# Third block's self-attention: two loops with the choice of queries between them, or one stream with the choice behind it

## The chip, the cores and the metric
The kernel runs on one core of one Trainium2 chip. A core has five engines with queues of their own: TensorE (PE in the profile, its weight loads PEld), VectorE (DVE), ScalarE (ACT), GpSimd (POOL) and SyncE (SP), which only starts DMAs here. The metric is the time of the whole kernel on the device, in microseconds: the median of three runs.

## The reference, cut to what matters
The network has twelve layers (four blocks of cross-attention, self-attention and feed-forward); x is 64 sequences of 32 tokens of 128 numbers. The layer in question adds to x the following, computed from the layer-normed x:

```python
Q, K, V = proj(wq, bq), proj(wk, bk), proj(wv, bv)        # 16 heads of 8
scores = jnp.einsum('bhqd,bhkd->bhqk', Q, K) * scale
u = min(L, max(1, int(np.log(L))))                        # 3 of 32 queries
top_u = jax.lax.top_k(scores.max(axis=-1), u)[1]          # the 3 with the highest maximum, per sequence and head
q_sel = jnp.take_along_axis(Q, top_u[..., None], axis=2)
attn = jax.nn.softmax(jnp.einsum('bhud,bhkd->bhuk', q_sel, K) * scale, axis=-1)
ctx = jnp.einsum('bhuk,bhkd->bhud', attn, V)
padded = zeros.at[bi, hi, top_u].set(ctx)                 # the other 29 queries give zero
return padded.transpose(0, 2, 1, 3).reshape(B, L, D) @ wo.T + bo
```

## The kernel before
All is float32. The 2048 tokens are 16 tiles of 128 rows (four sequences each) and four quarters of four tiles. Layers run one after the other. Every engine has its own program of the whole network, written out in order; between them stand counting semaphores (`T.done` counts one up, `T.due` lists what still has to be waited for). An engine takes its instructions strictly in order, so an instruction that waits holds everything behind it. At the end of a layer each engine drains, and the next layer begins when all have (`fence_before`). PSUM has eight banks of 512 columns; the dictionary `free` says for each bank which event must have come before PE writes it again.

The layer is `L2Attn` (line 2625). All projections and scores of a sequence and head are computed for all 32 queries, and the choice is a mask of zeros and ones.

Start (`start_pe`, line 589): PE turns the normed rows of quarters 0 to 2 (line 388), fills the gap until quarter 3 is normed with query projections (line 424, two passes per matmul), turns quarter 3, and projects the last quarter's queries and all keys. ACT empties the even quarters (line 438), DVE the odd ones (line 450).

First loop, 16 tiles: POOL spreads the keys of a tile by head (`pool_keys`, line 1670, four operations); PE computes the scores of 16 heads into four banks, two sets of banks in turn (`pe_scores`, line 1491, 32 passes); DVE takes the maximum over the keys (line 1552) and subtracts it (line 1555); ACT takes exp in place (line 1628); DVE adds up the weights (line 2708). The weights of all 16 tiles are kept.

Then the choice (line 2654 on): PE turns the 16 x 16 maxima of each row so that a partition holds (tile, head) and a row holds the 32 queries of a sequence; DVE copies them (line 2711) and finds the three highest in three rounds of six or seven small operations (`pick_dve`, line 508); takes the reciprocal of all 256 sums per row (line 2715); PE turns the mask back; DVE multiplies it into the reciprocals (line 2719).

Second loop, 16 tiles: POOL multiplies the weights by that gate (line 1678); ACT repeats the normed x of a sequence four times (line 1612); PE computes the values at full width, four matmuls into 512 columns (line 1505), turns the weights of a tile (line 1514) and averages (line 1524, 32 small passes); DVE adds the bias to the values and masks them (lines 1581 and 1585); ACT copies the turned weights (line 1635) and the average (line 1642). PE's order in a step is values of tile i, turn of tile i-1, average of tile i-2.

Output: PE multiplies by the output weights per quarter (line 460), DVE adds the bias (line 553) and adds to x (line 556).

`HeadStream` (line 1692) is the form that three other layers use: lines 1736 (scores), 1750 (values, 32 small passes straight into one row block per head), 1760 (turn), 1771 (average, with four more columns per group that give the sums of the weights), DVE 1805 and 1808, ACT 1849 (four copies of the values), 1874 (exp) and 1880 (copy of the turned weights), POOL 1894 (keys). In it a divided mean is turned back per tile (lines 1815, 1818, 1779, 1856).

Other lines that the prediction speaks of: 368 is a matmul that only keeps PE busy, 551 and 556 are additions to x.

Of the kernel before, what the change touches and what calls it, by code (L numbers as in the profile page):

```python
# [10 lines left out]
ALU = mybir.AluOpType  # L11
# [32 lines left out]
class Tally:  # L44
# [8 lines left out]
    def sem(self, name):  # L53
# [15 lines left out]
        "z": "lin_out", "z_out": "lin_out", "rows": "rows_out", "ffn_hidden": "lin_out", "products": "lin_out",  # L69
# [1383 lines left out]
class HeadAttention:  # L1453

    def __init__(self, g, tag, room, qT, kT, ready, xT, wv, scale, OT, *, key_mask=None, block=None, softcap=None,
                 bias_col=None, bias_row=None, repeated=None, keepall=False):
        self.g, self.tag, self.qT, self.kT, self.ready, self.xT = g, tag, qT, kT, ready, xT
        self.wv, self.scale, self.OT, self.key_mask, self.block = wv, scale, OT, key_mask, block  # L1460
        self.softcap, self.bias_col, self.bias_row, self.repeated = softcap, bias_col, bias_row, repeated
        self.keepall = keepall
        self.kB = [room.take(BT * HG * S) for _ in range(3)]
        if repeated is None:
            self.xR = [room.take(BT * HG * S) for _ in range(3)]
        self.pr = [room.take(H, S) for _ in range(NT if keepall else 3)]
        self.pT = [room.take(NG * P) for _ in range(2)]
        self.vB = [room.take(BT * D) for _ in range(3)]
        self.mx, self.sm = room.take(NT, H), room.take(NT, H)
        self.rest = room  # L1470

    def output(self, q):
        return "h_out", (self.tag, 4 * q + 3)

    def score_bank(self, i):
        return NG * (i % 2) if self.keepall else 0

    def tile(self, i):
        return self.repeated[i] if self.repeated is not None else self.xR[i % 3]

    def pe_scores(self, e, T, free, i):
        g, PS, at0 = self.g, self.g.PS, self.score_bank(i)
        for w in T.due(*free_of(free, at0), ("h_keys", (self.tag, i)), *self.ready(i // 4)):
            e.wait_ge(*w)
        for n in range(NG):
            r = slice(S * n, S * n + S)
            for b in range(BT):
                at = P * i + S * b  # L1490
                k = e.matmul(PS[S * b:S * b + S, at0 + n, 0:P], self.qT[r, at:at + S], self.kB[i % 3][r, P * b:P * b + P],
                             start=True, stop=self.key_mask is None)
        for n in range(NG if self.key_mask is not None else 0):
            k = e.matmul(PS[:, at0 + n, 0:P], self.block, spread(self.key_mask(i), [P, HG, S], 1), start=False, stop=True)
        k.then_inc(*T.done("h_scores", (self.tag, i)))
        free[at0] = ("h_less" if self.softcap is None else "h_tanh"), (self.tag, i)
        for n in range(1, NG):
            free[at0 + n] = free[at0]

    def pe_values(self, e, T, free, i):  # L1500
        PS, b, x = self.g.PS, 4 + i % 2, self.tile(i)
        for w in T.due(free[b], ("h_repeated", (self.tag if self.repeated is None else "shared", i))):
            e.wait_ge(*w)
        for j in range(BT):
            k = e.matmul(PS[:, b, D * j:D * j + D], x[:, P * j:P * j + P], self.wv, start=True, stop=True)
        k.then_inc(*T.done("h_values", (self.tag, i)))
        free[b] = ("h_biased" if self.bias_row is not None else "h_masked"), (self.tag, i)

    def pe_turn(self, e, T, free, i):
        PS, p = self.g.PS, self.pr[i % len(self.pr)].rearrange("p (g h) k -> p g (h k)", g=NG)  # L1510
        for w in T.due(free[6], ("h_normal", (self.tag, i))):
            e.wait_ge(*w)
        for n in range(NG):
            k = e.transpose(PS[:, 6, P * n:P * n + P], p[:, n, :], self.g.C["ident"])
        k.then_inc(*T.done("h_turned", (self.tag, i)))
        free[6] = ("h_pT", (self.tag, i))

    def pe_average(self, e, T, free, i):
        PS = self.g.PS
        for w in T.due(free[7], ("h_pT", (self.tag, i)), ("h_masked", (self.tag, i))):  # L1520
            e.wait_ge(*w)
        for j in range(BT):
            for n in range(NG):
                k = e.matmul(PS[S * n:S * n + S, 7, S * j:S * j + S], self.vB[i % 3][:, D * j + S * n:D * j + S * n + S],
                             self.pT[i % 2][:, P * n + S * j:P * n + S * j + S], start=True, stop=True)
        k.then_inc(*T.done("h_average", (self.tag, i)))
        free[7] = ("h_out", (self.tag, i))

    def pe(self, e, T, free, fill=None):
        for i in range(NT + 2):  # L1530
            if i < NT:
                self.pe_scores(e, T, free, i)
                self.pe_values(e, T, free, i)
# [3236 lines left out]
```

## Time and profile before

| what | value |
|---|---|
| timed runs | 2098.18, 2100.51, 2100.89 us; median 2100.51 |
| the profiled execution | 2076.97 us, span 2075.2 us |
| granted clock of TensorE, mean | 0.911 of 2.4 GHz |
| PE busy | 1733.9 us, 84% of the span |
| DVE busy | 1371.5 us, 66% |
| ACT busy | 1035.9 us, 50% |
| POOL busy | 916.9 us, 44% |
| DMA | 130.63 MB moved |
| first score of the layer | 987.41 us from the start of the span |
| its last addition begins | 1070.08 us |

The profile is of one execution. "Chain" is the chain of work that ended last, followed back from the last instruction; "issue" in it is time in which an engine waited for nothing that the profile shows. PE's granted clock has two levels here, 1.00 (2.4 GHz) and 0.50 (1.2 GHz); a number between them in a window means that it changed inside. A float32 matmul appears as two passes.

### The profile page before, as it was taken

To read this page: it belongs to the slowest core of one execution; us is meant where nothing else is said; L and a number is where in the kernel's file an instruction comes from. 1 tells how busy PE (TensorE), PEld (TensorE's weight loads), DVE (VectorE), ACT (ScalarE), POOL (GpSimd) and SP (SyncE) were. 2 spreads that over 40 slices of the span, in tenths; PEclk is the share of its full clock that TensorE was granted. 3 is DMA by queue.
4 is the path that set the end of the run, shared out by engine and by line. 5 is a ranking of instruction groups with operands and counts; after the bars stand their busy time and mean duration, and the time that the engine had idled before them with its cause. 6 is when DMAs were issued, how large, how long until landed. Compare 5 with 4: busy or idle time off the path is not lost.

```text
span 2075.2 us, 49700 instructions
## 1 busy us (share of the span) xinstructions
PE 1733.9 (84%) x19776; PEld 1173.8 (57%) x19776; DVE 1371.5 (66%) x3589; ACT 1035.9 (50%) x2670; POOL 916.9 (44%) x1092
## 2 busy tenths in 40 slices
PE   7678999999988789988387879999999997547596
PEld 4323556666654656654265756677766675125396
DVE  6799996576765555446883168666777866676622
ACT  4445664488864742233231346676766753115243
POOL 2243454556650624210533053216767668423543
PEclk9878999999999999999597989999999998766698
DMA  8000000100017100053004411100001000031187
GB/s 358 1 1 0 0 1 1 76 5 5 5 36 314 66 2 1 1 209 138 2 25 141 136 29 25 38 21 12 21 12 31 11 11 1 10 136 45 53 303 234
DMA packets 60424, 130.63 MB, mean 63 GB/s; under 512 B 16713, under 2 KB 38940, under 8 KB 54560
## 3 DMA queue, kind: packets, MB, share of 16 engines
q1 hardware_dynamic: 56896, 121.32, 16.2%
q0 software_dynamic: 3296, 6.12, 0.9%
q8 instruction: 157, 2.57, 0.5%
q14 instruction: 75, 0.61, 0.1%
HBM read 107.97 MB, written 20.12 MB: 62 GB/s over the span
## 4 chain that ended last, share of the span: by engine, by line
PE 54%; DVE 22%; issue 8%; ACT 7%; DMA 4%; POOL 3%; SPq 1%; POOLq 1%; DVEq 0%; ACTq 0%
PE PS L3254 4%; PE PS L2541 4%; PE PS L424 3%; PE PS L460 3%; PE PS L3301 3%; PE PS L3286 2%; PE PS L3285 2%; DMA arena<-in_ctx 2%; PE PS L3243 2%; PE PS L1760 2%; PE PS L2341 2%; PE PS L1736 2%; DVE arena L253 2%; PE PS L1082 1%; PE PS L3293 1%
## 5 line engine op out<-in xcount | busy, mean ns | idle before, releaser
L321 POOL TENSOR_TENSOR arena<-arena 128x4 f32<-128x4 f32 (+3 forms) x109 | 118.8, 1091 | 365.3 <-DVE arena L264 243.9
L3369 ACT ACTIVATE arena<-PS,arena 128x289 f32<-128x289 f32 x256 | 127.6, 503 | 73.5 <-DVE arena L3483 73.1
L3483 DVE TENSOR_REDUCE arena<-PS 128x1 f32<-128x289 f32 x256 | 113.6, 455 | 71.7 <-PE PS L3254 67.6
L3254 PE MATMUL PS<-arena 128*128 128x289 f32 x512 | 150.6, 417 | 10.4 <-ACT arena L3369 7.5
L1894 POOL TENSOR_TENSOR arena<-arena 128x128 f32<-128x128 f32 x384 | 140.4, 403 | 38.0 <-PE PS L1736 16.5
L1258 POOL TENSOR_TENSOR arena<-arena 128x512 f32<-128x512 f32 x64 | 85.0, 1328 | 110.0 <-DVE arena L1403 110.0
L1849 ACT COPY arena<-PS 32x128 f32<-32x128 f32 x384 | 99.5, 259 | 25.0 <-PE PS L1750 20.8
L3254 PEld LDWEIGHTS PS<-arena 128*128 128x128 f32 x512 | 87.5, 191 | 34.3 <-ACT arena L3369 16.7
L3212 POOL TENSOR_TENSOR arena<-arena 128x1024 f32<-128x1024 f32 x14 | 33.0, 2358 | 159.8 <-ACT arena L3360 159.8
L3497 DVE TENSOR_TENSOR arena<-PS,arena 128x580 f32<-128x580 f32 x128 | 97.6, 762 | 4.4
L368 PE MATMUL PS<-arena 128*128 128x512 f32 x158 | 82.6, 657 | 11.5 <-DVEq L4568 10.8
L2541 PE MATMUL PS<-arena 128*128 128x512 f32 x192 | 90.1, 604 | 0.0
L460 PE MATMUL PS<-arena 128*128 128x128 f32 (+4 forms) x576 | 83.5, 292 | 7.5 <-DVE arena L415 4.0
L460 PEld LDWEIGHTS PS<-arena 128*128 128x128 f32 (+1 forms) x576 | 78.8, 214 | 17.9 <-issue 4.6
L1398 DVE TENSOR_TENSOR_SCAN arena<-arena 128x512 f32<-128x512 f32 x64 | 85.2, 1331 | 0.0
L424 PE MATMUL PS<-arena 128*128 128x512 f32 x160 | 81.0, 625 | 4.8 <-DVE arena L415 4.0
L388 PE MATMUL PS<-arena 128*128 128x128 f32 x272 | 45.7, 311 | 42.5 <-DVEq L4568 10.4
L407 ACT COPY arena<-PS 128x512 f32<-128x512 f32 x40 | 23.2, 587 | 111.6 <-PE PS L388 111.4
L2361 POOL TENSOR_TENSOR arena<-arena 128x512 f32<-128x512 f32 x36 | 39.2, 1089 | 87.4 <-DVE arena L2355 68.8
L1115 PE MATMUL PS<-arena 128*128 128x512 f32 x128 | 75.8, 677 | 2.4 <-DVE arena L1382 2.4
L3267 PE MATMUL PS<-arena 128*128 128x128 f32 x512 | 69.8, 275 | 8.1 <-DVE arena L3497 7.9
L1071 PE MATMUL PS<-arena 96*128 96x512 bf16 x128 | 49.8, 433 | 31.1 <-DVE arena L1388 19.2
(453 smaller groups left out, 4818.1 us busy)
## 6 DMA issues: line engine op xcount, KB each, us to landing
arena<-in_ctx SPq DMA_DIRECT2D x32, 1091.0 KB, 10.4
arena<-in_f_w SPq DMA_DIRECT2D x39, 514.0 KB, 5.3
arena<-in_ctx SPq DMA_DIRECT2D x16, 834.0 KB, 16.8
lists<-arena SPq DMA_DIRECT2D x8, 1040.0 KB, 11.0
arena<-in_f_w SPq DMA_DIRECT2D x32, 256.0 KB, 2.9
arena<-in_ctx SPq DMA_DIRECT2D x16, 512.0 KB, 3.5
arena<-in_mid SPq DMA_DIRECT2D x1, 3796.5 KB, 12.3
arena<-in_late SPq DMA_DIRECT2D x1, 3204.0 KB, 11.6
```

Source lines behind the costliest of these rows:

```text
L321: e.tensor_tensor(x, x, half.broadcast_to(list(x.shape)), ALU.pow).then_inc(*T.done("norm_root", tag))
L424: e.matmul(g.PS[0:w_.shape[-1], b, :], w_, src[:, cut(q)], start=True, stop=True).then_inc(*T.done("lin_out", (tag, q)))
L460: i = e.matmul(g.PS[:, b, n * j:n * j + n], src[:, at:at + P], w_, start=True, stop=True)
L1258: e.tensor_tensor(u, u, g.XT[:, self.part(j)], ALU.mult).then_inc(*T.done("a0_u", j))
L1398: e.tensor_tensor_scan(self.Ur[:, j % R, :], self.Ar[:, j % R, :], self.Ur[:, j % R, :], 0.0, ALU.mult, ALU.add).then_inc(*T.done("a0_scan ...
L1849: k = e.copy(v[r, :, h, :], PS[r, 4, 0:P].rearrange("p (a d) -> p a d", d=HD))
L1894: k = e.tensor_tensor(dst[:, b], spread(src[:, b, :], [P, HG, S], 1), spread(self.g.C["headmask"], [P, HG, S], 2), ALU.mult)
L2541: e.matmul(g.PS[:, b, :], w_, g.XT[:, cut(q)], start=True, stop=True).then_inc(*T.done(name, k))
L3254: e.matmul(PS[:, b, 0:UL], self.qt[i % 2][:, j, P * k:P * k + P], self.kt[i % 3][:, j, :], start=True, stop=True).then_inc(*T.done("k3_sco ...
L3369: e.activation(self.weights(n, k, 0, UL), PS[:, self.score_bank(n, k), 0:UL], ACT.Exp, bias=self.st[:, h, k:k + 1], accum_out=self.st[:, h ...
L3483: e.tensor_reduce(self.st[:, n % 2, k:k + 1], PS[:, self.score_bank(n, k), 0:UL], AXX, ALU.max, negate=True).then_inc(*T.done("k3_least", ...
L3497: e.tensor_tensor(p, spread(over, [P, 2, UP], 2), p, ALU.mult).then_inc(*T.done("k3_normal", (n, k // 2)))
```

## The change
`HeadAttention`, which only this layer used, is taken out; a new class `HeadPicked` on top of `HeadStream` takes its place. One stream of 16 tiles does scores, values, exp, turn and average. The values get their bias from a matmul of the identity with a prepared bias tile, which opens the bank. The weights are neither normalised nor masked: the average and the four sums per group of heads are copied as they are into a kept array (`keep`). The maxima are kept for all tiles, and behind the stream come one turn of the maxima, the three rounds, a reciprocal of the kept sums, the product with the turned choice, and per quarter the product with the kept averages (`dve_mean`), a turn back, a copy and the output matmul. POOL adds the output bias to x during the stream. The key projection of quarter 0 is moved into the gap before the last quarter's transposes. Eight idle matmuls stand on PE between the stream and the turn of the choice.

```diff
+class HeadPicked(HeadStream):
+    def pe(self, e, T, free, more):
...
+        def values(m):
+            v = wv.rearrange("p (n h d) -> p h n d", n=NG, h=HG)
+            for w in T.due(free[4]):
+                e.wait_ge(*w)
+            e.matmul(PS[:, 4, 0:P], g.C["ident"], self.bias, start=True, stop=False)
+            for j in range(BT):
+                for h in range(HG):
+                    k = e.matmul(PS[S * h:S * h + S, 4, S * j:S * j + S].rearrange("p (n d) -> p n d", n=NG),
+                                 self.xT[:, P * m + S * j:P * m + S * j + S], v[:, h], start=False, stop=j == BT - 1)
...
+        def average(m):
+            v, p, w_ = self.vB[m % 3], self.pT[m % 2], self.WIDE
+            for w in T.due(free[7], ("h_pT", (tag, m)), ("h_masked", (tag, m)), ("h_cleared", tag)):
+                e.wait_ge(*w)
...
+            free[7] = ("h_kept", (tag, m))
+
+        for m in range(NT + 2):
+            if m < NT:
+                scores(m)
+                values(m)
+            if 0 <= m - 1 < NT:
+                turn(m - 1)
+            more(m)
+            if m >= 2:
+                average(m - 2)
...
+    def dve(self, e, T, more):
+        def less(m):
...
+            e.tensor_reduce(m4, sc, AXX, ALU.max).then_inc(*T.step())
...
+                            ALU.subtract).then_inc(*T.done("h_less", (tag, m)))
+        def keep(m):
+            for w in T.due(("h_average", (tag, m))):
+                e.wait_ge(*w)
+            e.tensor_copy(self.kept[:, m, :], PS[:, 7, 0:NG * self.WIDE]).then_inc(*T.done("h_kept", (tag, m)))
+        for m in range(NT + 2):
+            if m < NT:
+                less(m)
+            if m >= 2:
+                keep(m - 2)
+            more(m)
...
+    def dve_chosen(self, e, T, b):
...
+        e.reciprocal(share.rearrange("p t (n h) -> p (t n) h", n=NG), sums).then_inc(*T.step())
+        for w in T.due(T.prev(), ("h_sel_turned", self.tag)):
+            e.wait_ge(*w)
...
+        e.tensor_tensor(flat, flat, self.g.PS[:, b, 0:2 * P], ALU.mult).then_inc(*T.done("h_chosen", self.tag))
...
+    def act(self, e, T, more):
...
+        for m in range(NT + 2):
+            if m < NT:
+                values(m)
+                for w in T.due(("h_less", (tag, m))):
+                    e.wait_ge(*w)
+                e.activation(self.pr[m % 3], self.pr[m % 3], ACT.Exp, scale=self.scale).then_inc(*T.done("h_exp", (tag, m)))
+            if 0 <= m - 1 < NT:
+                for w in T.due(("h_turned", (tag, m - 1)), ("h_average", (tag, m - 3))):
+                    e.wait_ge(*w)
+                e.copy(self.pT[(m - 1) % 2], PS[:, 6, :]).then_inc(*T.done("h_pT", (tag, m - 1)))
...
 class L2Attn(Layer):
     def pe(self, e, T):
+        def first():
+            keys(range(1))
+            queries(range(NQ - 1))
+        def more(m):
+            if m == NT:
+                h.pe_best(e, T, free, 0)
+        self.start_pe(e, T, free, first)
         queries((NQ - 1,))
+        keys(range(1, NQ))
+        h.pe(e, T, free, more)
+        idle_pe(e, T, g, free, 3, 8)
+        h.pe_sel(e, T, free, 1)
+        for q in range(NQ + 1):
+            if q < NQ:
+                h.pe_back(e, T, free, q, 2 + q % 2)
+            if q:
+                out(q - 1, 3 + q)
     def pool(self, e, T):
+        def more(m):
+            if m in (1, 3, 5, 7):
+                x = quarter(g.X, m // 2)
+                e.tensor_tensor(x, x, spread(g.W["a2_bo"], [P, 4, D], 1), ALU.add).then_inc(*T.done("a2_added", m // 2))
     def dve(self, e, T):
+        def more(m):
+            if m == NT:
+                h.dve_best(e, T, 0)
+                h.dve_round(e, T, 0)
+        h.dve(e, T, more)
+        for i in range(1, self.KEEP):
+            h.dve_round(e, T, i)
+        h.dve_chosen(e, T, 1)
+        h.dve_mean(e, T, 0)
+        h.dve_mean(e, T, 1)
         for q in range(NQ):
+            add(q, 4 + q)
+            if q + 2 < NQ:
+                h.dve_mean(e, T, q + 2)
```

## Rows read from the trace of the kernel before
**Rows 1.** The page, chain that ended last, shares of the span by engine.
```profile
PE 54%; DVE 22%; issue 8%; ACT 7%; DMA 4%; POOL 3%; SPq 1%; POOLq 1%; DVEq 0%; ACTq 0%
```
**Rows 2.** Windows: us, busy (instructions) of PE, PEld, DVE, ACT, POOL, clock, DMA share, GB/s.
```profile
992.00:1018.00 26.00, 9.18 (x386) 3.74 (x386) 25.52 (x42) 8.51 (x14) 15.97 (x44) 0.50 0.01 2
1030.00:1035.00 5.00, 5.00 (x24) 5.00 (x25) 2.71 (x5) 0.65 (x2) 3.73 (x4) 0.50 0.00 0
1036.00:1064.00 28.00, 27.25 (x672) 23.98 (x674) 22.63 (x29) 17.08 (x42) 15.44 (x12) 1.00 0.01 3
```
**Rows 3.** Chain that ended last, in this layer: start us, us, what.
```profile
981.96 4.57 PE PS L424 x10
...
987.41 0.66 PE PS L1491 x28
...
1019.06 0.34 DVE arena L2711
...
1028.16 1.76 DVE arena L2715
...
1030.66 3.41 PE PS L1505 x16
...
1070.08 0.69 DVE arena L556
```
**Rows 4.** Lines 1552 and 1555: ns min/median/max, first and last start us.
```profile
L1552 DVE TENSOR_REDUCE arena<-PS x16: 681/682/694, 988.1 to 1016.3; 128x16 f32<-128x512 f32 x16
...
L1555 DVE TENSOR_TENSOR arena<-PS,arena x16: 692/693/695, 988.8 to 1017.0; 128x512 f32<-128x512 f32 x16
```
**Rows 5.** ACT's instructions in order, stream of the first block, full clock.
```profile
443.49 1.06 ACT L1849 COPY arena<-PS 32x128 f32<-32x128 f32 x4 [0.16 <-PE PS L1750]
444.58 0.63 ACT L1874 ACTIVATE arena<-arena 128x512 f32<-128x512 f32 x1
445.23 0.58 ACT L1880 COPY arena<-PS 128x512 f32<-128x512 f32 x1
...
445.91 1.06 ACT L1849 COPY arena<-PS 32x128 f32<-32x128 f32 x4
```
**Rows 6.** Chain that ended last, same stream, full clock.
```profile
510.47 0.40 PE PS L1771 x32
510.87 0.45 PE PS L1736 x31
...
511.91 0.39 PE PS L1750 x32
512.30 0.59 PE PS L1760 x4
```
**Rows 7.** Chain that ended last, stream of the last block, clock 0.50.
```profile
1871.71 0.64 PE PS L1771 x32
1872.35 0.68 PE PS L1736 x32
...
1873.89 1.46 issue
...
1875.88 1.05 PE PS L1760 x4
```
**Rows 8.** Chain: eight passes at full clock, four transposes at 0.50.
```profile
1064.24 1.10 PE PS L460 x8
...
1894.49 1.08 PE PS L388 x4
```
**Rows 9.** Windows around changes of the clock, columns as in rows 2.
```profile
1865.00:1870.00 5.00, 2.50 (x62) 1.23 (x49) 1.37 (x2) 2.24 (x6) 1.63 (x5) 0.52 1.01 418
...
1068.00:1071.00 3.00, 0.09 (x2) 0.11 (x2) 2.70 (x5) 0.00 (x0) 0.00 (x0) 1.00 0.00 0
1071.00:1085.00 14.00, 12.62 (x63) 7.66 (x63) 12.84 (x55) 1.60 (x4) 5.93 (x5) 1.00 0.01 2
...
1087.00:1090.00 3.00, 0.00 (x0) 0.00 (x0) 2.73 (x8) 0.00 (x1) 0.00 (x0) 0.50 1.02 294
```

More of the change, by code:

```diff
@@ L68 @@
         "last_turned": "cols_turned", "sel_turned": "cols_turned", "yturned": "cols_turned", "kc_out": "lin_out", "bc": "lin_out",
-        "z": "lin_out", "z_out": "lin_out", "rows": "rows_out", "ffn_hidden": "lin_out", "products": "lin_out",
+        "z": "lin_out", "z_out": "lin_out", "rows": "rows_out", "kept": "ms", "ffn_hidden": "lin_out", "products": "lin_out",
         "query_out": "lin_out", "located": "lin_out", "select": "cleared",
@@ L2636, in __init__ @@
         self.qT, self.kT, self.OT = room.take(NTOK), room.take(NTOK), room.take(NTOK)
-        self.heads = HeadAttention(g, 7, room, self.qT, self.kT, lambda q: [lin("a2_q", q), lin("a2_k", q)], g.XT, W["a2_wvT"],
-                                   float(np.float32(1.0) / np.sqrt(np.float32(HD))), self.OT, bias_row=W["a2_bv"], keepall=True)
-        self.best, self.sel = room.take(2 * BT, S), room.take(2 * BT, S)
-        self.pick_room = Region(g.arena, room.at, room.hi)
-        room.take(1200)
-        self.tmp = [room.take(4, D) for _ in range(2)]
+        self.heads = HeadPicked(g, 7, room, [(self.qT, self.kT, lambda q: [lin("a2_q", q)], lambda q: [lin("a2_k", q)], W["a2_wvT"], None)],
+                                g.XT, float(np.float32(1.0) / np.sqrt(np.float32(HD))), self.OT, self.KEEP, W["a2_bv"])
     def pe(self, e, T):
@@ L2674, in act @@
         self.start_act(e, T)
+        lin_act(e, T, g, "a2_k", self.kT, range(4), W["a2_bk"], (0,))
         lin_act(e, T, g, "a2_q", self.qT, range(4, 8), W["a2_bq"])
-        lin_act(e, T, g, "a2_k", self.kT, range(4), W["a2_bk"])
-        for i in range(NT):
-            h.act_exp(e, T, i)
-        for i in range(3):
-            h.act_repeat(e, T, i)
-        for i in range(NT + 2):
-            if 3 <= i + 2 < NT:
-                h.act_repeat(e, T, i + 2)
-            if 0 <= i - 1 < NT:
-                h.act_turned(e, T, i - 1)
-            if i >= 2:
-                h.act_out(e, T, i - 2)
+        lin_act(e, T, g, "a2_k", self.kT, range(4), W["a2_bk"], (2,))
+        h.act(e, T, lambda m: None)
+        for q in range(NQ):
+            h.act_out(e, T, q, 2 + q % 2)
     def pool(self, e, T):
-        h = self.heads
+        g = self.g
         self.start_pool(e, T)
-        for i in range(NT):
-            h.pool_keys(e, T, i)
-        for i in range(NT):
-            h.pool_normal(e, T, i, ("a2_chosen", 0))
+        def more(m):
+            if m in (1, 3, 5, 7):
+                x = quarter(g.X, m // 2)
+                e.tensor_tensor(x, x, spread(g.W["a2_bo"], [P, 4, D], 1), ALU.add).then_inc(*T.done("a2_added", m // 2))
+        self.heads.pool(e, T, more)
     def dve(self, e, T):
@@ L4726 @@
         "a2_woT": a["L2_attn_wo"].T, "a2_bq": col(a["L2_attn_bq"]), "a2_bk": col(a["L2_attn_bk"]),
-        "a2_bv": row(a["L2_attn_bv"]), "a2_bo": row(a["L2_attn_bo"]), "f2_gwT": a["L2_ffn_gate_w"].T,
+        "a2_bv": np.broadcast_to(a["L2_attn_bv"].reshape(NG, HG, HD).transpose(1, 0, 2)[:, None, None], (HG, S, BT, NG, HD)).reshape(P, P), "a2_bo": row(a["L2_attn_bo"]), "f2_gwT": a["L2_ffn_gate_w"].T,
         "x3_g1": row(a["L3_xattn_ln1_g"]), "x3_b1": row(a["L3_xattn_ln1_b"]), "x3_g2": row(a["L3_xattn_ln2_g"]),
```

385 lines of the change are left out of this document (139 added, 246 removed).

## The prediction
> **What bounds the kernel now.** I read the chain of waits first, then cut the stage of this layer (984 to 1071 us) out of it. Over the whole kernel the chain lies on PE for about half and on DVE for a fifth [rows 1], so each stage has its own limit and the layer has to be read alone. Nothing is in flight for a later layer while it runs and all engines meet at its end, so what it saves moves everything behind it forward one for one.
>
> The windows show three of the layer's pieces [rows 2]. In 992:1018 DVE is busy 25.5 of 26 us and PE 9.2 of 26: the score loop is bound by DVE, and its granted clock has sunk to 0.50 (1.2 GHz). In 1030:1035 PE is full but still at 0.50. In 1036:1064 PE is busy 27.3 of 28 us at 1.00 (2.4 GHz): the value loop is bound by PE. Between 1018 and 1030 the chain lies on DVE alone [rows 3]. So two loops of 16 tiles, each with one full engine and others half idle, stand one behind the other, with a serial choice of queries between them. The chain shows the seams [rows 3]: last projections from 981.96, the choice from 1019.06, a reciprocal of 256 columns at 1028.16, values from 1030.66, the last addition at 1070.08. From the first score (987.41) to the end of that addition (1070.77) are 83.4 us.
>
> **The change part by part.** Removed: per tile the DVE sum over 512 columns, ACT's copy that repeats x four times, eight full-width value passes on PE, two DVE passes over the values, POOL's product of 512 columns with the gates. None is a term by itself; what counts is the length of the new schedule.
>
> *Head.* The last stretch of projections is ten passes, five matmuls, 4.57 us [rows 3]. The key projection of quarter 0 now goes ahead of the last transposes, where PE waits anyway. One of five leaves the queue: 0.9 us. First score at 986.5. POOL clears three value buffers first, in time in which it waited before.
>
> *Stream, per tile.* DVE: the maximum and the subtraction are 0.68 and 0.69 us [rows 4], the copy of 144 columns into the kept array about 0.3 (nearest row: 0.34 on the path for 256 columns [rows 3]): 1.7. ACT does what it does in the stream of the first block: four copies of 32 partitions 1.06, exp 0.63, copy of the transposed weights 0.58, with gaps of some 0.02 between [rows 5]: 2.34 without the small output copy, which is now gone from the stream. PE at 2.4 GHz, by its steps on the chain of that stream: scores 0.45, values 0.39, transposes 0.59, average 0.40 [rows 6]; new is one matmul of two passes that puts the bias into the bank. Bounds: 0.03 (two of the 32 small passes of the values [rows 6]) and 0.91 (a projection over 512 columns, 4.57 for five [rows 3]), which would make PE the bound at 2.9 and cost 0.5 a tile, 8 in all; eight passes of 128 columns take 1.10 [rows 8], so two take 0.27, and I take that because it is the same shape. PE 2.10. The loop between the engines: ACT's copy of tile m-2 frees bank 6, then PE turns, averages, scores, adds bias and values before ACT can go on: 2.10 and three hand-overs of about 0.05, 2.25. ACT's 2.34 is the longest. The stream of the first block, where PE had 2.42 of work, ran a tile in 2.42 (values copies at 443.49 and 445.91 [rows 5]); small fetch gaps come on top of 2.34, so I take 2.40. POOL makes four key products a tile in three buffers, as in that stream, and now also adds the output bias to x, a quarter every second tile; the stream of the first block gives it more than that to do, so I cost it at nothing, and it takes one of two DVE passes per quarter out of the tail. Were POOL late by one addition, the next scores would be late by about 1 us.
>
> The wait that is added: scores and averages now stand on one queue, so average m-2 waits for ACT's copy and, being in order, holds back scores m+1. That is in the loop above. The copy to the kept array stands in front of the next maximum on DVE but ends before those scores do.
>
> *Fill.* From the first score: scores, bias, values on PE 1.25, ACT copies and exp 1.7, then 0.3 of waiting since one set of score banks lets scores 1 start only after the subtraction of tile 0, then one ACT round 2.34: 5.6 us, to 992.1. Fourteen more rounds at 2.40: 33.6, to 1025.7.
>
> *Choice.* Last transposes, the transposes of the maxima and average 14 take 1.5, two kept copies 0.6, the copy and three rounds as before 9.1 (1019.0 to 1028.16 [rows 3]), reciprocal 1.76, product with the turned choice 0.45, first product for the means 0.7. To 1039.9. The eight idle matmuls are hidden under the rounds (16 passes of 512 columns at 0.46 each [rows 3], 7.3 us, over by 1034.5). The turning of the choice now goes beside the reciprocal instead of after it.
>
> *Tail.* Four times transposes, ACT copy, output matmuls, addition; but the DVE queue holds mean 2 behind addition 0, mean 3 behind addition 1, and PE's back-transposes of quarter 2 stand in front of output 1, so it is nearly serial: back 0, back 1, output 0, addition 0, mean 2, back 2, output 1, addition 1, mean 3, back 3, output 2, output 3, addition 3. At 2.4 GHz with 0.6, 1.1 and 0.7 for back, output and DVE [rows 3, 6, 8] this adds to 10.4 us; at 1.2 GHz with 1.08 for four transposes [rows 8] and half of 3.41 for eight passes [rows 3] to 14.7 us. The clock decides which. PE is idle, but for two short transposes, from about 1034.5 to 1039.9. In this trace the clock had fallen by 1087 after PE's work ended at about 1085, while an idle stretch of 2.9 us in 1068:1071 let it stand [rows 9]. Five microseconds are nearer to the first: I take 14.7. End at 1054.6 instead of 1070.8.
>
> **Sum: 16.1 us saved.** The profiled execution took 2076.97 us (span 2075.2), so it would be 2060.9. The three timed runs have their median at 2100.51, 23.5 higher, with nothing in the profile that says where; I take the difference off the median: 2084.4. A clock that is low at the end slows the next layer's start: PE is busy 12.6 of the 14 us behind the fence [rows 9], so 5 us at half rate cost 2.5 less the 1.4 idle, 1.1 at most. With half of that I put 2085.
>
> **The clock, row and rule.** The row: with PE busy a third of the time the clock is 0.50 through the score loop, and a full PE in 1030:1035 still ran at 0.50 before it came back [rows 2]. The new stream has PE at 2.1 of 2.4 us, so I hold it at 1.00. The Trainium skill, "TensorE: Matmul & The Clock Gate", section "A second HAM failure mode: psum-queue depth-cycling", speaks against this change: a kernel that goes round through its PSUM banks with small idle pauses between groups of matmuls sees its clock swing between the two levels. By that rule the stream would run at 1.2 GHz in part or throughout, and that is the second rival below, priced from rows.
>
> **Rivals.**
> *Tail at full clock.* The idle matmuls and the two transposes hold the clock: 20.4 us saved, 2080. For it: the gap behind 1068 [rows 9]. Against: the gap here is twice as long. Chance 0.23.
> *Slow stream, slower than before.* Place: scores 1 to average 15. At 1.2 GHz the stream of the last block shows scores 0.68, average 0.64, transposes 1.05 [rows 7]; values, scaled like the average, about 0.6; with a bias of 0.43 (a quarter of half of 3.41 [rows 3]) PE needs 3.4 us a tile and is the bound instead of ACT. That stream ran 1865:1870 at about 0.5 [rows 9] and also stood 1.46 us in an issue gap [rows 7]. If the clock falls in the fill (scores 0 and 1 with an idle pause between them) and stays there, 14 tiles cost 14 more, the fill and the last tile 2, and four such gaps 5.8: 21.8 against 16.1, 5.7 slower, 2106. It decides only if practically all tiles are slow; for it stands that the same sequence of work did fall there; against it that a full PE came back within about 5 us here [rows 2], and that DMAs, which had a share of 1.01 in that stretch [rows 9], are at 0.01 in this layer [rows 2]. Chance 0.05.
> *A low spell of 3 to 6 tiles, then full clock.* Costs 3 to 6: saving 10 to 13, 2089. Chance 0.25.
> *The stream does not overlap as written:* a tile takes 3.1 or more because ACT, DVE and PE wait in turn (turn waits for exp and for bank 6, average for the kept copy). 0.75 times 14 is 10.5, leaving 5.6 or less: 2095 to 2101, no difference that can be told at the low end. Against it: the same queues run 2.42 in the first block. Chance 0.07.
> My forecast has 0.40.
>
> **How the numbers follow.** 2085 is the forecast. The range takes in the full-clock tail and half of the next layer's uncertainty below (2077) and the low spell and the better half of the poor overlap above (2096). A measurement of this kernel can tell about 0.2%, 4.2 us. Faster than that: forecast, both clock cases around it and most of the rest, 0.90. Within it: the end of the poor overlap and a partly slow stream, 0.05. Slower: 0.05.
>
> **What would show it.** Right: copies of values on ACT every 2.3 to 2.5 us, ACT busy over 90% in the stream, the clock at 1.00 from 987 to beyond 1034; the last average about 1027; the reciprocal about 1037; back-transposes of about 1.1 us for four if the tail is slow, 0.6 if not; the next layer's fence near 1055. Wrong: PE as the engine that releases ACT's value copies, score passes at 0.68 for a tile through the stream, an issue gap of over 1 us, DVE idle before the kept copy for longer than 0.7 us a tile, or a layer that ends early while the kernel does not.

## The result, and the profile after

Twelve runs of each kernel on one chip: before 2095.86 us (2093.19 to 2100.89), after 2085.65 us (2072.25 to 2090.97), ratio 0.9938, 95% interval 0.9923 to 0.9954. By the ratio that is 13.0 us less (9.6 to 16.1) on 2095.86; the two medians lie 10.2 apart. The forecast was 2085.0, with a range of 2077 to 2096.

The profiled execution of the changed kernel took 2082.68 us (span 2080.9), 5.7 more than the profiled one of before. So the pair of profiles can't be subtracted as a whole; it has to be read stage by stage. From the first score to the end of the last addition: 83.4 us before [rows 3], 73.4 after (989.99 to 1063.39). From the end of VectorE's drain in front of the layer to the end of its drain behind it: 95.1 and 84.4, so 10.7 less. What made up for it lies in layers that the change doesn't touch. Between the same drains the last layer took 224.7 us before and 239.0 after, the third layer of the first block 229.3 and 233.6. The same program profiled once more (e1 below) gave 226.1 for the former and 234.5 for the latter, so the first is scatter between runs. The second is open: 231.7 to 236.8 in all thirteen profiles with the changed layer, against a single profile of before.

The page of the changed kernel, chain by engine, answers to [rows 1]. "Issue" stands at 14% for 8%, but that says little of the change: the chain of this one profile has a stretch of 113.86 us in the last layer in which it names no engine, and e1, the same kernel, shows 9%.

```profile
PE 54%; DVE 17%; issue 14%; ACT 7%; DMA 3%; POOL 2%; SPq 2%; POOLq 1%; DVEq 0%; ACTq 0%
...
1852.29 113.86 issue
```

Windows of the changed kernel (us; busy and instructions of PE, PEld, DVE, ACT, POOL; clock; DMA share; GB/s), as [rows 2]: the stream, the idle matmuls under the choice, the pause behind them, the tail.

```profile
996.00:1032.00 36.00, 31.17 (x1292) 22.12 (x1292) 21.03 (x38) 29.76 (x78) 18.39 (x45) 1.00 0.02 5
1037.00:1045.00 8.00, 7.54 (x48) 3.32 (x48) 7.45 (x20) 0.00 (x0) 0.00 (x0) 1.00 0.00 0
1047.00:1049.00 2.00, 0.00 (x0) 0.00 (x0) 1.93 (x3) 0.00 (x0) 0.00 (x0) 0.84 0.00 0
1049.00:1061.00 12.00, 9.06 (x39) 8.25 (x40) 3.30 (x6) 2.35 (x4) 0.00 (x0) 0.50 0.00 0
```

In the stream no engine is full: PE 87%, ACT 83%, DVE 58%. The clock stands at 1.00 there and falls in the pause before the tail. What fills the rest is in the chain that ended last (start us, us, what), which answers to [rows 3]:

```profile
989.09 0.89 issue
...
1002.13 0.45 issue
...
1005.31 0.95 issue
...
1016.10 0.98 issue
...
1019.94 0.65 issue
...
1030.43 0.99 issue
...
1046.26 1.67 DVE arena L1844
...
1049.17 1.97 PE PS L1771 x8
1051.13 1.91 PE PS L460 x8
...
1062.70 0.69 DVE arena L2677
```

In the first issue gap VectorE evicts the last projection (989.13 to 989.88). The five in the stream, 4.0 us, are something else, as the same chain shows when only 998 to 1010 is asked for: the gap of 0.95 us cuts the 32 score passes of one tile in two, behind the 26th, and no semaphore stands there.

```profile
1004.90 0.41 PE PS L1699 x26
1005.31 0.95 issue
1006.26 0.41 PE PS L1699 x6
1006.67 0.42 PE PS L1709 x2
```

Two groups by line, duration in ns as min/median/max: ScalarE's value copies and the bias matmul, both to be held against the forecast.

```profile
L1868 ACT COPY arena<-PS x64: 268/273/279, 991.4 to 1033.9; 32x128 f32<-32x128 f32 x64
...
L1709 PE MATMUL PS<-arena x32: 275/326/377, 990.4 to 1032.3; 128*128 128x128 f32 x32
```

### The profile page after: what moved, and what is told of

The parts are those of the page before. It is cut to its first block, busy times and chain, and to the rows that moved or that the text cites. A ratio compares the mean times of both kernels' runs of the same rounds, so it can differ in the third digit from the quotient of the medians.

```text
span 2080.9 us, 50581 instructions
## 1 busy us (share of the span) xinstructions
PE 1751.4 (84%) x20224; PEld 1179.2 (57%) x20224; DVE 1344.6 (65%) x3557; ACT 1044.3 (50%) x2706; POOL 902.1 (43%) x1086
## 3 DMA queue, kind: packets, MB, share of 16 engines
q1 hardware_dynamic: 56896, 121.32, 16.4%
## 4 chain that ended last, share of the span: by engine, by line
PE 54%; DVE 17%; issue 14%; ACT 7%; DMA 3%; POOL 2%; SPq 2%; POOLq 1%; DVEq 0%; ACTq 0%
PE PS L3224 4%; PE PS L2515 4%; PE PS L424 3%; PE PS L3271 3%; PE PS L3256 2%; PE PS L3255 2%; PE PS L3213 2%; PE PS L460 2%; PE PS L2315 2%; PE PS L1521 2%; PE PS L4222 2%; DMA arena<-in_ctx 2%; PE PS L4231 2%; PE PS L1497 1%; PE PS L1082 1%
## 5 line engine op out<-in xcount | busy, mean ns | idle before, releaser
L1655 POOL TENSOR_TENSOR arena<-arena 128x128 f32<-128x128 f32 x448 | 163.9, 404 | 52.8 <-PE PS L1497 16.0
L3224 PE MATMUL PS<-arena 128*128 128x289 f32 x512 | 150.7, 417 | 10.7 <-ACT arena L3339 7.7
L368 PE MATMUL PS<-arena 128*128 128x512 f32 x174 | 93.3, 674 | 9.5 <-DVEq L4538 8.8
L460 PE MATMUL PS<-arena 128*128 128x128 f32 (+4 forms) x576 | 86.7, 297 | 12.9 <-ACT arena L4272 5.4
L2515 PE MATMUL PS<-arena 128*128 128x512 f32 x192 | 90.6, 607 | 0.0
L424 PE MATMUL PS<-arena 128*128 128x512 f32 x160 | 80.4, 623 | 4.2 <-DVE arena L415 3.3
L388 PE MATMUL PS<-arena 128*128 128x128 f32 x272 | 46.2, 313 | 39.8 <-DVEq L4538 10.4
L1115 PE MATMUL PS<-arena 128*128 128x512 f32 x128 | 75.7, 676 | 2.4 <-DVE arena L1382 2.4
L2335 POOL TENSOR_TENSOR arena<-arena 128x512 f32<-128x512 f32 x36 | 39.2, 1090 | 87.1 <-DVE arena L2329 68.6
L1497 PE MATMUL PS<-arena 32*32 32x128 f32 x3072 | 58.4, 297 | 22.1 <-DVE arena L1569 11.0
## 6 DMA issues: line engine op xcount, KB each, us to landing
arena<-in_mid SPq DMA_DIRECT2D x1, 3796.5 KB, 12.6
```

What stands on the lines that cost most here:

```text
L368: e.matmul(g.PS[:, b, :], g.C["ident"], g.const_words[:, 0:512], start=True, stop=True)
L424: e.matmul(g.PS[0:w_.shape[-1], b, :], w_, src[:, cut(q)], start=True, stop=True).then_inc(*T.done("lin_out", (tag, q)))
L460: i = e.matmul(g.PS[:, b, n * j:n * j + n], src[:, at:at + P], w_, start=True, stop=True)
L1655: k = e.tensor_tensor(dst[:, b], spread(src[:, b, :], [P, HG, S], 1), spread(self.g.C["headmask"], [P, HG, S], 2), ALU.mult)
L2515: e.matmul(g.PS[:, b, :], w_, g.XT[:, cut(q)], start=True, stop=True).then_inc(*T.done(name, k))
L3224: e.matmul(PS[:, b, 0:UL], self.qt[i % 2][:, j, P * k:P * k + P], self.kt[i % 3][:, j, :], start=True, stop=True).then_inc(*T.done("k3_sco ...
```

## The experiments

Three theories are named in what was expected. A: TensorE's work sets the stream's tile. B: ScalarE, or the hand-over between it and TensorE, does. C, formed after the first four runs: the supply of TensorE's instructions does.

In each profile three stretches are measured. Stream: first score to the transposes of the last tile. Choice: from there to the end of the first product for the means. Tail: from there to the end of the last addition. "Low" is how long in the stretch, in all, the granted clock stood at 0.50. "Blocks" are 16384-byte packets of the DMA queue named instruction within the stream, and their mean distance in us. "Passes" are TensorE passes per tile; each has its weight load, so 102 passes are 204 instructions. The time is that of the one profiled execution, for e11 and e12 the median of six.

| kernel | passes | stream (low) | blocks, every | choice | tail (low) | layer | time |
|---|---|---|---|---|---|---|---|
| changed | 102 | 45.5 (0) | 12, 3.67 | 13.7 | 14.3 (12.9) | 73.4 | 2082.68 |
| e1 the same again | 102 | 47.4 (6.8) | 12, 3.87 | 13.7 | 11.0 (3.4) | 72.1 | 2074.34 |
| e2 no bias | 100 | 46.7 (11.5) | 12, 3.91 | 14.6 | 12.3 (6.8) | 73.5 | 2066.28 |
| e3 half the value copies | 102 | 46.1 (0) | 12, 3.78 | 13.7 | 11.1 (3.1) | 70.9 | 2070.37 |
| e4 warm tail | 102 | 46.8 (6.8) | 12, 3.78 | 14.1 | 10.3 (0) | 71.2 | 2077.25 |
| e5 few instructions | 72 | 39.1 (3.4) | 9, 4.16 | 13.7 | 11.1 (3.4) | 63.9 | 2057.82 |
| e6 small matmuls | 134 | 61.9 (13.7) | 16, 3.78 | 13.7 | 14.1 (12.5) | 89.7 | 2085.49 |
| e7 wide matmul | 104 | 47.1 (0) | 12, 3.72 | 13.7 | 12.3 (6.8) | 73.0 | 2070.43 |
| e8 head undone | 102 | 48.1 (6.8) | 12, 3.95 | 13.7 | 10.1 (0) | 71.9 | 2069.17 |
| e9 values in four | 84 | 47.5 (0) | 10, 4.47 | 13.7 | 12.2 (6.8) | 73.4 | 2069.73 |
| e10 tail | 102 | 48.0 (6.8) | 12, 3.92 | 14.1 | 7.3 (0) | 69.5 | 2077.75 |
| e11 tail again | 102 | 46.9 (0) | 12, 3.82 | 12.6 | 7.2 (0) | 66.6 | 2066.08 |
| e12 e11, values in two | 86 | 44.3 (0) | 10, 4.08 | 12.6 | 8.4 (3.4) | 65.3 | 2064.22 |

The time column can't judge an edit of this size: e1 is the changed kernel and stands 8.3 us from its other profile. The stretches can.

**e1: unchanged.** 

> The changed kernel once more, unchanged. First score to the end of the layer's last add was 73.4 us in the profile at hand, the tile period in the stream (from the scores of tile 3 to those of tile 15) 2.89 us. Both theories: the layer within 1 us of 73.4, the period 2.80 to 2.95. The gaps of 0.4 to 1.0 us of TensorE inside the stream, which no semaphore ends, come again in like number (four to six), but need not stand at the same tiles. Layers that the change doesn't touch may differ by several us from the profile at hand (the last block's by up to 10), which would say that one pair of profiles can't measure 13 us of the whole kernel.

72.1 for 73.4, tile period 3.05 for 2.89. Both differences have a name in the windows: the stream has a low spell of 6.8 us that the other profile lacks, and the tail has one of 3.4 us in place of 12.9. So the clock behind the choice isn't a property of the program. Windows of e1 from 1055 (us, PE busy, clock, DMA share, GB/s):

```profile
1055.00:1057.00 2.00, 1.21 (x7) 0.84 0.00 0
1057.00:1059.00 2.00, 2.00 (x11) 0.50 0.00 0
1059.00:1061.00 2.00, 0.62 (x5) 0.81 0.00 0
1061.00:1063.00 2.00, 1.15 (x11) 1.00 0.00 0
```

**e2: no bias.** Part left out: the bias of the values.

```diff
-            e.matmul(PS[:, 4, 0:P], g.C["ident"], self.bias, start=True, stop=False)
...
-  v[:, h], start=False, stop=j == BT - 1)
+  v[:, h], start=True, stop=True)
```

> The value matmuls start their bank themselves, and the bias matmul (two instructions, 0.42 us) is gone from each of 16 tiles; the values lack their bias. Theory A (TensorE sets the tile: its matmuls of 2.26 us plus gaps of about 0.4 us while it waits for instructions): the period falls from 2.89 to 2.45 to 2.55 us, where ScalarE's 2.4 us takes over, and the layer is 5 to 7 us shorter, 67 to 68. Theory B (ScalarE or the hand-over between ScalarE and TensorE sets the tile): period 2.80 or more, the layer at most 1.5 us shorter.

Theory A falls: the stream stayed at 46.7. Its low spells muddy that, but from 1012.43 to 1029.13, at full clock, six tiles took 2.78 us each and not 2.45 to 2.55, with PE 75% and ACT 80% busy in e2's window:

```profile
1012.00:1028.00 16.00, 12.07 (x598) 8.57 (x591) 8.98 (x17) 12.74 (x34) 5.90 (x16) 0.98 0.02 5
```

**e3: half the value copies.** Part left out: the values of head groups 2 and 3.

```diff
-            for h in range(HG):
+            for h in range(2):
                 r = slice(S * h, S * h + S)
                 k = e.copy(v[r, :, h, :], ...)
```

> ScalarE copies the values of two of the four head groups and leaves the other two out (they stay zero in the averages): its work per tile falls by 2 x 0.27 = 0.54 us, TensorE's is the same. Theory A: the period stays at 2.8 to 2.95 us and the layer within 1.5 us of 73.4. Theory B: the period falls by up to 0.54 to some 2.4 us, the layer by 6 to 8.6 us.

Theory B falls too: ScalarE has 0.54 us less per tile, 8.6 in all, and the stream is 46.1. Neither the busy time of PE nor that of ACT sets the stream. What all these profiles share are twelve blocks of instructions in the stream. This is the DMA view of the changed kernel for 990 to 1035 (queue and kind: packets, MB, share):

```profile
q8 instruction: 12, 0.20, 1.8%
```

The trace holds 3128 matmul and weight-load records in the stream and twelve blocks, 261 to a block. The score loop of the kernel before needed far fewer; its DMA view for 990 to 1016:

```profile
q8 instruction: 4, 0.07, 0.9%
```

That gave theory C: TensorE consumes instructions faster than they arrive. The first three tile periods average 2.33 us, on what had been fetched ahead, the later ones 2.89.

The traces bear it out gap by gap. In the changed kernel's profile the five gaps of the stream come after 885, 1139, 1900, 2153 and 2914 matmul and weight-load records, counted from the first score: always 253 or 254 apart, or three times that, so they cut the work where a block ends and not where a tile does. e3, e11 and others show gaps after the same counts. Windows of the changed kernel around its second gap: the transfer of a block, the gap, the transfer of the next (last column, GB/s):

```profile
1003.70:1004.90 1.20, 1.20 (x73) 0.95 (x67) 0.95 (x2) 0.89 (x4) 1.16 (x4) 1.00 0.06 14
...
1005.31:1006.26 0.95, 0.00 (x1) 0.00 (x1) 0.00 (x0) 0.93 (x2) 0.00 (x0) 1.00 0.00 0
...
1007.30:1008.30 1.00, 1.00 (x60) 0.79 (x45) 0.82 (x2) 0.72 (x3) 1.00 (x4) 1.00 0.06 16
```

The ten profiles whose streams issue 100 or more passes a tile have 69 issue gaps of over 0.3 us in the stream. 66 of them end 1.19 to 1.58 us after the transfer of a block has ended, and the next transfer begins 1.06 to 1.78 us after the gap's end. So TensorE has one block ahead of it at most, and the next is under way only once it has begun on the block before.

The Trainium skill, "Runtime: NRT & Kernel Launch", section "Instruction fetch mechanics", has the same unit, blocks of 16 KiB or 256 instructions fetched by the sequencer's own DMA queue while it works on the page before; the trace agrees on that. It calls the cost of a block boundary mostly hidden. Here the trace disagrees: gaps of 0.45 to 0.98 us stand at five of the boundaries.

**e4: warm tail.**

```diff
-        idle_pe(e, T, g, free, 3, 8)
+        idle_pe(e, T, g, free, 3, 10)
         h.pe_sel(e, T, free, 1)
+        idle_pe(e, T, g, free, 6, 2)
```

> Ten idle matmuls instead of eight ahead of the transposes of the selection (4 passes of 0.45 us more), and two (1.8 us) between those and the first transposes back, where TensorE stood 2.41 us and the clock fell. If the clock is kept: transposes of 0.55 for 1.11 us and rows of 0.9 to 1.0 for 1.7 to 1.9 us; four transposes and four rows in the chain, 4 x 0.5 + 4 x 0.9 = up to 5.6 us, of which some 4 stand in the serial chain, so the end of the sel transposes to the last add is 3 to 4.5 us shorter than the 14.2 of now; stream as in e1. Rival: the waits of 1.4 us between the rounds of the tail pull the clock down all the same, and the gain is under 1.5 us, or the added matmuls delay the transposes they stand before and eat it.

The tail is 10.3, 4.0 under the changed kernel's profile, at full clock throughout; the forecast's own sum for a full clock was 10.4. But e1, without the edit, has 11.0, so most of the time it is worth less than 4, and 0.5 went back into the choice.

**e5, e6, e7: the number of instructions alone.** In e5 the sixteen value matmuls are left out and the values are twice the bias. e6 and e7 add work that nobody reads.

```diff
 e5, for the loop of sixteen:
+            k = e.matmul(PS[:, 4, 0:P], g.C["ident"], self.bias, start=False, stop=True)
 e6, ahead of the bias:
+            for j in range(BT):
+                for h in range(HG):
+                    e.matmul(PS[S * h:S * h + S, 5, ...], self.xT[...], v[:, h], start=True, stop=True)
 e7, ahead of the bias:
+            e.matmul(PS[:, 5, 0:P], g.C["ident"], self.bias, start=True, stop=True)
```

> The sixteen value matmuls of a tile (32 columns each; 32 passes, 0.39 us together) are left out, and one more bias matmul of 128 columns (2 passes, 0.42 us) stands in their place: the values are twice the bias. TensorE's busy time per tile is the same, but it runs 72 passes with their weight loads instead of 102. Theory C, formed on the first four runs (the stream waits for instructions: TensorE's come in blocks of 16384 bytes, twelve of them in the 46 us of the stream, one per 3.5 to 3.9 us, and the first three tiles, which run on what was fetched ahead, need 2.15 to 2.3 us each): 72/102 of the blocks, so the supply would allow 2.1 us per tile, the period falls to the 2.3 to 2.5 that ScalarE needs and the time from the first score to the last tile's turn from 46.6 (mean of five profiles) to 38 to 41 us; blocks come at 3.7 to 4.5 us. Theory A (TensorE's busy time): no change, 45.5 to 47.5. Theory B (ScalarE): no change.

> Sixteen more value matmuls per tile, of 32 columns, into a bank that nobody reads: 32 more passes, 0.39 us of TensorE. Theory C: 134 passes with their loads for 102, so 2.9 x 134/102 = 3.8 us per tile, first score to last turn 57 to 62 us. Theory A: at most 16 x 0.39 = 6.2 us more, 51 to 53. Theory B: 46 to 48.

> One more bias matmul per tile into a bank that nobody reads: 2 more passes, 0.42 us of TensorE, the counterpart of e6 with the same time and almost no instructions. Theory C: 104 passes for 102, 46.5 to 48.5 us from first score to last turn. Theory A: 16 x 0.42 = 6.7 us more, 51 to 54.

All three went by theory C: 39.1, 61.9 and 47.1 us. e6 and e7 add the same TensorE time, 0.39 and 0.42 us a tile; one costs 16.4 over the profile of the changed kernel, the other 1.6. In e5 one matmul of 0.42 us stands for sixteen of 0.39 together, and the stream is 6.3 shorter; its blocks come every 4.16 us, so the queue waits for TensorE now and not the reverse. Window of e5, with ACT at 96%:

```profile
994.00:1022.00 28.00, 25.98 (x864) 18.75 (x864) 20.22 (x37) 26.95 (x74) 18.67 (x46) 1.00 0.02 4
```

Chain of e6: the gaps again cut groups of passes in two, and after one of 1.72 us the transposes take 1.05 for 0.59, at the low clock. So a fetch gap can cost twice; it need not, since the clock stood at 1.00 all through the stream of e3, which has gaps of 1.22 and 1.26 us.

```profile
1008.47 0.38 PE PS L1718 x28
1008.85 1.72 issue
1010.57 0.23 PE PS L1718
1010.80 1.05 PE PS L1728 x4
...
1017.08 0.28 PE PS L1718 x17
1017.36 0.86 issue
1018.22 0.33 PE PS L1718 x15
```

Its window there:

```profile
1010.00:1014.00 4.00, 3.43 (x102) 2.52 (x103) 0.98 (x2) 2.31 (x6) 0.62 (x2) 0.58 0.02 4
```

**e8: the head undone.**

```diff
         def first():
-            keys(range(1))
             queries(range(NQ - 1))
...
-        keys(range(1, NQ))
+        keys(range(NQ))
```

> The first quarter of the key projection is put back behind all of the query projection, on TensorE and on ScalarE, as in the kernel before; the stream and the tail stay. From the first of the layer's transposes to the first score: 10.90 us in the changed kernel's profile, 11.61 in the profile of before. If the move of the projection is what gained there: 11.5 to 12.5. Rival: the start of the stream hangs on something else (GpSimd's clearing of the value buffers, the keys), and it stays within 0.2 us of 10.9.

11.61 us for 10.89 from first transposes to first score: the move is worth 0.72, exactly what before and after differ by.

**e9: the values in four matmuls.**

```diff
-            e.matmul(PS[:, 4, 0:P], g.C["ident"], self.bias, start=True, stop=False)
             for j in range(BT):
-                for h in range(HG): ...
+                e.matmul(PS[:, 4, D * j:D * j + D], self.xrep(m)[:, P * j:P * j + P], wv, start=j == 0, stop=False)
+            for h in range(HG):
+                k = e.matmul(own[r, :, h, :], g.C["ident"][:, r], self.bias..., start=False, stop=True)
```

> The same results with fewer instructions: VectorE repeats a tile's columns of x four times into the unused normalised rows (one copy of 128x512 per tile, three tiles ahead), four matmuls of 128 columns make the values in place of sixteen of 32, and the bias comes in by four matmuls on the head groups' own columns: 84 passes with their loads per tile for 102. Theory C: the supply allows 84/102 of the 2.89 to 3.05 us seen, 2.4 to 2.5; ScalarE needs 2.33, VectorE 1.69 plus the copy, which is under 0.7 if it goes like VectorE's other 128x512 passes: period 2.4 to 2.6 us, first score to last turn 40 to 43 for 46 to 48.5, the layer 5 to 7 us shorter. Rival: the copy makes VectorE the bound, with the subtraction late for ScalarE, or it takes over 1 us; then the period is 2.8 or more and nothing is gained.

A miss for both: the copy took 0.42 us and no gap is left, yet nothing was gained. TensorE itself is full (window of e9):

```profile
994.00:1030.00 36.00, 36.00 (x1035) 26.75 (x1037) 23.59 (x48) 28.80 (x75) 18.59 (x45) 1.00 0.02 4
```

PE in order of time: eight full-width passes take 1.16 us where 32 narrow ones took 0.39, whose records overlap (each of them lasts 0.20 us by the groups by line).

```profile
1012.98 0.52 PE L1699 MATMUL PS<-arena 32*32 32x128 f32 x32
1013.42 1.16 PE L1712 MATMUL PS<-arena 128*128 128x128 f32 x8
1014.51 0.43 PE L1716 MATMUL PS<-arena 128*32 128x128 f32 x8
1014.87 0.66 PE L1725 MATMUL PS<-arena 128*128 128x128 f32 x4
```

**e10, e11: the tail.**

```diff
         for q in range(NQ):
+            if q + 2 < NQ:
+                h.dve_mean(e, T, q + 2)
             add(q, 4 + q)
-            if q + 2 < NQ:
-                h.dve_mean(e, T, q + 2)
...
 in the stream, for m in (6, 10, 14): reciprocal of the sums of tiles m - 6 to m - 3; four tiles left behind the choice
 idle matmuls: e10 ten and two as e4, e11 eight and one
```

> Stream as it is; three edits behind it: the warm matmuls of e4; VectorE's reciprocal of the sums done for twelve tiles within the stream and only for the last four behind the choice (1.75 us to about 0.5); and the third and fourth average made ahead of the first and second residual add instead of behind them, so that their transposes stand right behind the rows before. Last turn to the layer's last add was 24.0 us in e4 (with its tail at full clock): 1.2 us less by the reciprocal, 2 to 2.5 less by the order, 20 to 21. Rival: the adds, now behind an average each, are the bound in their place and the order gains under 1 us: 22 to 23. The three short reciprocals in the stream cost nothing if VectorE has its half microsecond of slack per tile: first score to last turn 46 to 48.5 as before.

> e10 with eight idle matmuls for ten ahead of the selection's transposes (in e10 they ended at 1055.4, where the choice had been ready since 1053.7, and gave back what the moved reciprocal gained) and one for two behind them. The stream is the changed kernel's. Last turn to the end of the first average 11.8 to 12.4 us for 13.3, from there to the last add 7.3 to 8.5 (7.34 in e10, 10.1 to 14.3 in the eight profiles with the tail of now), so some 6 us less than the changed kernel; that was 13.0 us under the kernel before, which makes 18 to 20 of 2096: ratio 0.9900 to 0.9920. Rival: without the second idle matmul the clock falls in the tail, 9.5 to 11 us for 7.3, and the ratio is 0.9925 to 0.9940.

The tail fell to 7.3 and 7.2: the order alone is worth 3 us against e4. In e10 the choice stayed at 14.1, because the queue had been filled for too long. The idle passes took 10.55 us, some at low clock, and the choice, ready at 1053.7, waited for them (PE of e10):

```profile
1044.99 10.55 PE L368 MATMUL PS<-arena 128*128 128x512 f32 x20
1055.37 0.38 PE L1763 MATMUL PS<-arena 128*128 128x128 f32 x2
```

With eight, e11 gets 12.6 (11.8 to 12.4 were expected), and a ratio of 0.991 (0.9881 to 0.9939), as forecast. The chain of e11 ends:

```profile
1050.13 0.70 DVE arena L1862
...
1050.88 0.67 PE PS L1771 x4
1051.57 0.60 ACT arena L1894
...
1052.21 1.17 PE PS L460 x8
...
1055.41 1.85 PE PS L460 x16
1057.28 0.69 DVE arena L2686
```

**e12: e11 and the values in two column halves.**

```diff
+            e.matmul(PS[:, 4, 0:2 * P]..., g.C["ident"], own, start=True, stop=False)
             for j in range(BT):
+                for u in range(2):
+                    k = e.matmul(PS[2 * S * u:2 * S * u + 2 * S, 4, ...], self.xrep(m)[:, 2 * S * j:2 * S * j + 2 * S], v[:, u], ...)
```

> e11, and the values by eight matmuls of 64 columns of weights (VectorE repeats the tile's columns of x twice, 128x256) and one bias matmul of 256 columns: 86 passes with their loads per tile for 102, and not the full-width passes of e9, whose eight took 1.16 us. Theory C: 86/102 of 2.97 (mean period of six profiles of the stream as it is) is 2.5 us per tile where TensorE's work is under that: its sum is 0.45 + 0.6 + 0.5 + 0.59 + 0.41 = 2.55 with the new bias and values guessed between e9's and the present ones. Period 2.5 to 2.65, first score to last turn 41 to 44 us for 46 to 48.5, 4 to 6 us under e11, ratio 0.9875 to 0.9900. Rival, as in e9: passes with wider weights no longer run beside one another, values 0.8 us or more, period 2.8 to 2.9 and no difference to e11.

Tile period 2.69 for a forecast of 2.5 to 2.65, the stream 44.3 for 41 to 44: between the forecast and its rival, and the window again has PE full. Ratio 0.9904 (0.988 to 0.9928), not to be told from e11.

```profile
1004.00:1040.00 36.00, 36.00 (x1139) 25.33 (x1138) 25.97 (x55) 31.07 (x81) 18.81 (x46) 1.00 0.02 5
```

By the ratios both e11 and e12 beat the kernel before, by 19 and 20 us of 2084.13, the median of eleven runs of it beside theirs. Against the changed kernel their layer is 6.8 and 8.1 us shorter by the profiles; the intervals of the three ratios overlap.

## Why the prediction was right, and where it wasn't

**The sum.** 16.1 us were forecast for the layer, 10.7 came in the profile: 10.0 behind the first score and 0.7 ahead of it. The kernel's 13.0 measured us lie between. That is right for a partly wrong reason, since what was too fast in the stream was set against a tail priced at its worst, where most runs are better. And 10.7 is what the rival with a low spell had priced (10 to 13), but it came by another cause.

That the time itself, 2085.65, came out 0.65 from the forecast is luck. The forecast took 15.5 us off a median of three runs, 2100.51. The median of the twelve runs is 2095.86, and 15.5 off that would be 2080.4, 5 us under what was measured, though still in the range.

**Head.** 0.9 forecast, 0.72 measured, alone in e8.

**Stream.** The step that failed is "small fetch gaps come on top of 2.34, so I take 2.40": it took the supply of instructions for a trifle, and it was the bound. The tile took 2.89, the stream 45.5 us for a forecast of 39.2, and 45.5 to 48.1 in all nine profiles whose stream issues 100 to 104 passes. ScalarE's 2.34 was right as a floor: e5 ran at 2.33 a tile and 39.1 in all, the forecast's number, once instructions were no limit. The five gaps make 4.0 of the 6.3 us over; how the other 2.3 divide was not taken apart. The mistake is in the row. [rows 5] shows two copies 2.42 apart; over the 64 tiles of that stream the subtractions stand 3.1 us apart (407.6 to 603.2 in the kernel before), and its DMA view for 415 to 540 already has 34 blocks in 125 us, one per 3.7, the rate that bound the new stream:

```profile
q8 instruction: 34, 0.56, 1.8%
```

That stream carries projections as well, so I had put the difference down to those. The limit was visible, and counted in instructions the forecast would have been 204 / 256 x 3.7 = 2.9 us a tile. Of its own signs two spoke against the forecast, ACT busy 83% where over 90 were asked, and a tile of 2.89 for 2.3 to 2.5; the sign that would have named the cause, an issue gap of over 1 us, just failed to come in this profile (0.98) and came in e1 (1.22).

**Bias.** 0.27 forecast, 0.42 on the chain; its rows show 0.33 for a pass. What it cost can't be told from scatter: with two passes fewer (e2) or more (e7) the stream took 46.7 and 47.1, within the 45.5 to 48.1 of the same stream unchanged.

**Clock in the stream.** 1.00 to beyond 1034 in this profile, as forecast. Five of the nine profiles with 100 to 104 passes a tile spent 6.8 to 11.5 us of the stream at 0.50, so the rival of a low spell is real; but with the stream waiting for instructions it costs about 1 us (46.7 to 48.1 with a spell, 45.5 to 47.1 without) and not 3 to 6. By the rule of the Trainium skill that was cited, "TensorE: Matmul & The Clock Gate", section "A second HAM failure mode: psum-queue depth-cycling", the clock would swing between its levels; the traces agree in so far, in five of the nine. That the whole stream runs slow, the rival's condition, which the page does not state, came in no run.

**Choice.** 14.2 forecast, 13.7 in nearly all profiles.

**Tail.** 14.7 at 1.2 GHz forecast, 14.3 in the profile; 10.4 at 2.4 GHz, 10.3 in e4. Both prices hold. The condition was met in this profile: PE was idle, but for the transposes of the choice, from 1044.70 to 1049.17 (1.61 and 2.41 us), 4.5 us for a forecast of 5.4, and the clock fell at 1048.4. But the pause of 2.41 us stands in every profile of this tail and doesn't always lead to the same clock: the tail had 12.9, 3.4, 6.8 and 0 us at 0.50 in profiles of the same tail. The rival with full clock, put at 0.23, is part of the truth in most runs.

**The profiled pair.** That the whole profile came out 5.7 longer while the kernel is 13 shorter comes from layers elsewhere, most of it from scatter in the last one (14.3). The ratio gives 2.3 more than this layer shows. Its interval, 9.6 to 16.1, takes in the 10.7, so nothing has to be explained; runs with a shorter tail than the profiled one (e1: 3.3) could be a part of it, but that was seen in single profiles only.

## What to carry to other kernels

Where a stage is made of many small matmuls, count TensorE's instructions per unit of work (passes and weight loads both) and compare with the fastest steady rate of instruction blocks in the trace, here 256 per 3.7 us; it is a bound like an engine's busy time, and no engine's row shows it. Take a unit's price from the mean period of a stream, not from its best pair. Merging small matmuls pays only as far as they did not already run beside one another: 84 and 86 passes gained 0 and 2.6 us where 5 to 7 and 4 to 6 were expected.

## What was not expected of the hardware

- TensorE's instructions arrived in blocks of 16384 bytes, on average 3.67 to 3.82 us from one to the next in the streams of 102 to 104 passes that kept the full clock (single distances 3.3 to 4.6). Where TensorE stood still for a block, its transfer had taken 0.88 to 1.43 us, the first instruction ran 1.19 to 1.58 us after the transfer's end, and the next transfer began 1.06 to 1.78 us after that. The medians, 1.11, 1.37 and 1.22, make 3.70 us, which is the distance of the blocks. So the rate is set by the way round this loop, and the transfer is less than a third of it. What the other two parts consist of, the traces don't show.
- What is fetched ahead is little. When the first gap came in the changed kernel, 12.1 us into the stream, 885 matmuls and weight loads had run since the first score. The transfers begun at 992.3 and 996.3 are used up in them; the one begun at 1000.2 is what the gap waited for. 885 less two blocks of 254 such records leaves 377, one and a half blocks, that had stood ready at the first score.
- Behind the same pause of 2.4 us the same tail spent between 0 and 12.9 us at the low clock.
- A VectorE copy of 128x512 within the working memory took 0.42 us, the subtraction of the same size out of the matmul banks 0.69 (e9).
